# Regrouping the down side's high product by 32 copies inside the on-chip memory, in place of sixteen turnings on TensorE

## The chip, the cores and the metric

The kernel runs on one core of a Trainium2 chip. The metric is the device time of one execution in microseconds (us), lower is better. TensorE (PE) multiplies, VectorE (DVE), ScalarE (ACT) and GpSimd (POOL) do the rest, and SyncE (SP) issues most of the DMA transfers. A change of less than 0.3% of the time is within what repeated measurements of this kernel can tell from no change.

## The reference, cut to what matters

```
def butterfly(y, weights, dim):            # 11 stages for dim 2048
    for stage in range(weights.shape[0]):
        s = 2 ** stage
        nb = dim // (2 * s)
        yr = y.reshape(*lead, nb, 2, s)
        a, b = yr[..., 0, :], yr[..., 1, :]
        w = weights[stage].reshape(nb, s, 2, 2)
        y = jnp.stack([w00 * a + w01 * b, w10 * a + w11 * b], axis=-2).reshape(*lead, dim)
    return y
...
h = einsum('bsd,dh->bsh', layernorm(x), W_exp) + b_exp
h = butterfly(h, up_weights, 2048)
h = gelu(h + up_bias)
h = butterfly(h, down_weights, 2048)
y = einsum('bsh,hd->bsd', h, W_con) + b_con + down_bias
```

x has shape (32, 512, 512). Ahead of this stands a gate: x is multiplied, after a layernorm, by a decaying running sum of the squared context, and added to x. Both butterflies are linear, so the kernel folds them once, at its start, into the two weight matrices: the up side into W_exp, the down side into W_con. The change touches the folding of the down side alone.

## The kernel before, in words

The kernel has two parts. The **folding** makes W1 (the up side) and W2 (the down side), both split into a rounded high half and a low remainder, so that three fast products give nearly the precision of fp32. The **main loop** then runs over 16 pairs of token blocks (`supers`), each with 8 steps `p` of 7 products by W1 (`product`, line 1916 of the profile) and the down products by W2 (`down_a`, line 1937, and `down_b`, line 1950). The first step of the first pair, `p = 0`, is woven into the end of the folding.

A butterfly of 11 stages is a product by a "low" matrix (7 stages, inside a block of 128 features) and one by a "high" matrix (4 stages, across the 16 blocks). On the down side W_con comes into the tile `wcon` with its rows in the order that the high product needs: partition (k e), slot r, for feature 128k + 16e + r. The folding steps are listed in `FOLD`; each makes one PSUM bank of 128x512 on PE (`fold_step` of the tensor block), which ACT or DVE then evicts to the place that `kept` names. Four banks are used in turn, so a step waits until the one four places ahead of it in `FOLD` is evicted. The steps that matter here are:

- `turn_high` (4 steps, line 1816) turns the down side's high matrix in `HX[:, 1]`.
- `high_dn` (16 steps, line 1818) multiplies `wcon[:, r]` by it, four products of 128 columns for each r, with W_con as the stationary side. The result is W_con turned, d on the partitions, and ACT scatters it into `Z` (viewed as `Zd`).
- `back` (16 steps, line 1824) turns each block k of `Zd` back, and the eviction writes it over `wcon[:, k]`: now the partition is the feature inside block k. These are the sixteen turnings.
- `turn_low` (4 steps, line 1820) turns the low matrix `LX[:, 1]`.
- `low_dn` (16 steps, line 1803, in the order `W2_ORDER`) multiplies block k by it. ACT rounds the result (`w2_slot`, line 992), DVE makes the remainder (line 1341), and SP stores the pair to HBM (`store_w2`, line 634).
- `bias_low` and `bias_turn` (lines 1792 and 1798) fold the biases; POOL goes on from them.
- `tokens` (8 steps, line 1822) turns the first eight 128-row blocks of normalised tokens into `raw`. DVE makes the tokens' sums in `raw` (`token_sum`, line 1462), ACT rounds a half of `raw` into a place of `xop` (`tokens_hi`, line 1040), DVE makes its remainder (`tokens_lo`, line 1445), and `product` reads both.

The tiles of the folding and those of the main loop share memory: the seven places of `xop`, 8 KB of each partition, lie over `Z` (places 0 to 3, four r each), over `HX` (4 and 5) and over `LX[:, 0]` (6). W1's own first two steps are staged in `w1_first`, a place of `xop` and `w1r` (`weights_hi`, line 1022), and SP stores them to HBM with `store_w1` (line 623), three groups for each of the two. `w1_first` lies under `raw`, so ACT waits for the stores of groups 0 and 1 before it evicts the first `tokens`.

What sets the order is the text of each engine's program, its semaphores, and SP's one queue, which issues the transfers in program order and stands still at each wait.

Of the kernel before, what the change touches and what calls it, by code (L numbers as in the profile page):

```python
# [24 lines left out]
def xattn_ffn_program(nc, x_in, ctx_in, w_exp, b_exp, up_w, up_bias, down_w, w_con, b_con, down_bias, out):  # L25
# [31 lines left out]
    XORDER = (0, 1, 3, 2, 5, 4, 6)  # L57

# [6 lines left out]
    W2_ORDER = (2, 3, 4, 5, 6, 7, 12, 13, 8, 1, 9, 0, 14, 10, 11, 15)  # L65
    W2_USE = [(i, 0) for i in range(14)] + [(3, 1), (14, 0)]
# [16 lines left out]
    with es:  # L83
# [122 lines left out]

        low_loaded = [sem("low_up_loaded"), sem("low_dn_loaded")]
# [118 lines left out]
        FOLD += [("high_dn", r, "act") for r in range(4)]  # L326
        FOLD += [("bias_low", 0, "act")]
        FOLD += [("high_dn", r, "act") for r in range(4, 8)]
        FOLD += [("bias_turn", 0, "act")]
        FOLD += [("high_dn", r, "act") for r in range(8, R - 3)]  # L330
        FOLD += [("tokens", i, "act") for i in range(2)]
        FOLD += [("high_dn", r, "act") for r in range(R - 3, R)]
        FOLD += [("tokens", i, "act") for i in range(2, J)]
        FOLD += [("turn_low", q, "act") for q in range(KH // 4)]
# [85 lines left out]
        Zd = Z[:, :, :].rearrange("p a b -> p (a b)").rearrange("p (c h) -> p c h", c=KD)  # L420

        def kept(kind, i, bank):
# [13 lines left out]
            if kind == "turn_high":  # L436
                return HX[:, 1, 4 * i:4 * i + 4, :].rearrange("p a b -> p (a b)"), whole
            if kind == "high_dn":
                return Zd[:, :, :].rearrange("p c (k r e) -> p c k r e", k=KH, r=R)[:, :, :, i, :],\
                    whole.rearrange("p (c k e) -> p c k e", c=KD, e=E)  # L440
# [3 lines left out]
            if kind == "tokens":  # L444
                return raw[:, i // J, :, :].rearrange("p c (g j i) -> p c g j i", g=G, j=J)[:, :, :, i % J, :],\
                    whole.rearrange("p (c g i) -> p c g i", c=KD, g=G)
            assert kind == "back"
            return wcon[:, i, :], whole
# [121 lines left out]
        def _(sp):  # L570
# [48 lines left out]
            def store_w1(n):  # L619
                p = W1_ORDER[n]  # L620
                for g, (m0, m1) in enumerate(GROUPS):
# [19 lines left out]
            store_w1(0)  # L641
# [338 lines left out]
        def _(act):  # L980
# [43 lines left out]
            def tokens_hi(u, m, first):  # L1024
                if not first:
                    act.wait_ge(m_done, u * PER + (m + 1 - NM))
                if m in (0, 1):
                    if first:
                        act.wait_ge(fold_made, fold_at("back", KH - 1) + 1)
# [10 lines left out]
                act.activation(xop[:, XPOS[m], 0, :, :], x_source(m), ACT.Copy).then_inc(xhi_ready, 1)  # L1040
# [48 lines left out]
            fold_step("high_dn", 3)  # L1089
            fold_step("bias_low", 0)  # L1090
            for r in range(4, 8):
                fold_step("high_dn", r)
            fold_step("bias_turn", 0)
            for r in range(8, 12):
                fold_step("high_dn", r)
            fold_step("high_dn", 12)
            for group in range(2):
                act.wait_ge(w1_stored[0][group], NX)
            for i in range(2):
                fold_step("tokens", i)  # L1100
            for r in range(13, R):
                fold_step("high_dn", r)
            for i in range(2, J):
                fold_step("tokens", i)
            for q in range(KH // 4):
                fold_step("turn_low", q)
            for k in range(4):
                fold_step("back", k)
            for k in range(4, 10):
                fold_step("back", k)  # L1110
            for i in range(J, J + 2):
                fold_step("tokens", i)
            for k in (10, 12, 14, 15):
                fold_step("back", k)
            tokens_hi(0, 0, True)
            tokens_hi(0, 1, True)
            for k in range(4):
# [123 lines left out]
        def _(dve):  # L1241
# [73 lines left out]
            def top_products(dn):  # L1315
                dve.wait_ge(path_product, spreads(dn, LOWS - 1))
                for c, bank in enumerate(TOP_PLACE[dn]):
# [3 lines left out]
                    if dn:  # L1321
                        last = nc.vector.tensor_tensor(
                            out=whole.rearrange("p o (r a e) -> p o a e r", r=R, a=2),
                            in0=paths.rearrange("p (o e r) -> p o e r", o=KH // 4, r=R).unsqueeze(2)
                            .to_broadcast([P, KH // 4, 2, E // 2, R]),
                            in1=coef.rearrange("p o a (e r) -> p o a e r", r=R), op=ALU.mult)
                    else:
                        last = path_stage(nc.vector, flat(whole), paths, coef, LOW - 1)
# [114 lines left out]
            def tokens_lo(u, m):  # L1443
                dve.wait_ge(xhi_ready, u * NM + (XPOS[m] + 1))
                nc.vector.tensor_tensor(out=xop[:, XPOS[m], 1, :, :], in0=x_source(m),  # L1445
                                        in1=xop[:, XPOS[m], 0, :, :].bitcast(f32), op=ALU.subtract).then_inc(xlo_ready, 1)
# [61 lines left out]
            for k in (11, 13):  # L1508
                fold_step("back", k)
            for i in range(J + 2, 2 * J):  # L1510
                fold_step("tokens", i)
            tokens_lo(0, 0)
            tokens_lo(0, 1)
            token_sum(0, 0, first=True)
            for k in range(2):
                fold_step("low_dn", k)
            token_sum(0, 1)
# [183 lines left out]
        def _(pe):  # L1701
# [73 lines left out]
            def fold_step(kind, i):  # L1775
# [24 lines left out]
                if kind == "low_dn":  # L1800
                    k = W2_ORDER[i]
                    wait_kept(pe, "back", k)
                    nc.tensor.matmul(bank[:, :], LX[:, 1, k, :], wcon[:, k, :], start=True, stop=True)\  # L1803
                        .then_inc(fold_made, 1)
                    return
                if kind == "tokens":
                    pe.wait_ge(xn_ready, i + 1)
                for c in range(4):
# [8 lines left out]
                    elif kind == "high_dn":  # L1817
                        last = nc.tensor.matmul(o, wcon[:, i, block_c], HX[:, 1, i, :], start=True, stop=True)  # L1818
# [4 lines left out]
                    elif kind == "back":  # L1823
                        last = nc.tensor.transpose(o, Zd[:, c, i * P:(i + 1) * P], ident[:, :])  # L1824
# [36 lines left out]
            for r in range(R):  # L1861
# [4 lines left out]
                if r == 3:  # L1866
                    fold_step("bias_low", 0)
                if r == 7:
                    fold_step("bias_turn", 0)
                if r == R - 4:  # L1870
                    for i in range(2):
                        fold_step("tokens", i)
            for i in range(2, J):
                fold_step("tokens", i)
            pe.wait_ge(low_matrix_ready, 2)
            for q in range(KH // 4):
                fold_step("turn_low", q)
            wait_kept(pe, "high_dn", R - 2)
            wait_kept(pe, "high_dn", R - 1)
            for k in range(KH):  # L1880
                if k == 10:
                    for i in range(J, J + 2):
                        fold_step("tokens", i)
                fold_step("back", k)
            for i in range(J + 2, 2 * J):
# [161 lines left out]
```

## Time and profile before

| | |
|---|---|
| median of 3 runs | 2752.51 us (2751.94 to 2758.26) |
| profiled execution, its time | 2752.11 us |
| profiled execution, its span | 2750.4 us |
| PE busy | 2728.7 us, 99% of the span |
| DVE, ACT, POOL busy | 2119.6, 1132.2, 427.1 us |
| first step of the main loop that stands free of the folding (`product(1, 0)`) | starts at 139.64 us |

The span is cut by the profiler from the first to the last instruction; the execution's time is 1.7 us longer. PE is busy nearly everywhere, so what counts is when it gets to the main loop proper, and whether it waits after that.

### The profile page before, as it was taken

Reading aid. Unit: us, or ns where it says so; the run is one execution under the profiler, and the core shown is the slowest. Engines: PE = TensorE matmul, PEld = TensorE weight load, DVE = VectorE, ACT = ScalarE, POOL = GpSimd, SP = SyncE. Lnnn points to the kernel's source line nnn. Section 1 sums busy time; section 2 is a strip of 40 time slices with the busy share of each in tenths; the row PEclk is TensorE's granted clock in tenths of the full one; section 3 lists DMA queues with packets and bytes.
Section 4 is the critical chain, followed back from the end, with each engine's and each line's share of the span. In section 5 each row is a group of like instructions: output and inputs, shape, how many; then the busy total and the mean of one; then the engine's idle time right before and its main releaser. Section 6 shows DMA issues by size and latency. Waiting matters only on the chain.

```text
span 2750.4 us, 35138 instructions
## 1 busy us (share of the span) xinstructions
PE 2728.7 (99%) x12168; PEld 2251.9 (82%) x12168; DVE 2119.6 (77%) x3544; ACT 1132.2 (41%) x1731; POOL 427.1 (16%) x608
## 2 busy tenths in 40 slices
PE   8999999999999999999999999999999999999998
PEld 6788888888888888888888888888888888888887
DVE  8888887877878777787877788787787877778533
ACT  5754434344343433434343343434334343343432
POOL 5356010110101011020111101011010101102000
PEclk8999999999999999999999999999999999999999
DMA  9675956657585675857657585675758567585543
GB/s 274 244 235 171 281 165 198 200 170 224 155 231 177 181 220 161 241 153 216 194 168 222 152 249 165 194 202 171 223 156 235 172 189 213 161 242 153 187 146 100
DMA packets 288373, 535.76 MB, mean 195 GB/s; under 512 B 36854, under 2 KB 98454, under 8 KB 271046
## 3 DMA queue, kind: packets, MB, share of 16 engines
q1 hardware_dynamic: 281808, 531.05, 64.1%
q10 hardware_dynamic: 5414, 1.25, 0.3%
q8 instruction: 99, 1.62, 0.2%
q0 software_dynamic: 976, 1.22, 0.2%
q14 instruction: 76, 0.62, 0.1%
HBM read 437.96 MB, written 63.96 MB: 182 GB/s over the span
## 4 chain that ended last, share of the span: by engine, by line
PE 98%; DVE 1%; ACT 0%; issue 0%; DMA 0%; POOL 0%; DVEq 0%
PE ps L1916 44%; PE ps L1937 25%; PE ps L1950 25%; PE ps L1814 1%; PE ps L1710 1%; PE ps L1782 0%; PE ps L1818 0%; PE ps L1812 0%; PE ps L1824 0%; DMA wexp<-in_L_ffn_W_exp_dram 0%; PE ps L2022 0%; PE ps L1803 0%; DVE raw L1462 0%; DVE xop L1445 0%; PE ps L1729 0%
## 5 line engine op out<-in xcount | busy, mean ns | idle before, releaser
L1916 PE MATMUL ps<-xop,w1r 128*128 128x512 f32 x5376 | 1366.1, 389 | 2.4 <-DVE xop L1445 2.4
L1916 PEld LDWEIGHTS ps<-xop,w1r 128*128 128x128 f32 x5376 | 1009.0, 188 | 215.2 <-DVE xop L1445 3.4
L1937 PE MATMUL ps<-w2r,ghi 128*128 128x512 f32 x2048 | 630.5, 389 | 0.0
L1950 PE MATMUL ps<-w2r,ghi 128*128 128x512 f32 x2032 | 625.7, 389 | 1.1 <-DVE x L1544 1.1
L1127 ACT ACTIVATE st<-ps 128x512 f32<-128x512 f32 x384 | 229.6, 598 | 820.0 <-PE ps L1916 819.9
L1544 DVE TENSOR_TENSOR x<-ps,x 128x512 f32<-128x512 f32 x508 | 348.4, 686 | 275.1 <-PE ps L1950 272.7
L1937 PEld LDWEIGHTS ps<-w2r,ghi 128*128 128x128 f32 x2048 | 384.4, 188 | 79.9 <-DVE w2x L1341 0.2
L1950 PEld LDWEIGHTS ps<-w2r,ghi 128*128 128x128 f32 x2032 | 381.3, 188 | 81.0 <-DVE x L1544 2.0
L1562 DVE TENSOR_TENSOR g<-ps,st 128x512 f32<-128x512 f32 x384 | 262.5, 684 | 211.7 <-PE ps L1916 211.7
L1131 ACT ACTIVATE g<-g,gelu_bias 128x512 f32<-128x512 f32 x384 | 275.5, 717 | 353.0 <-DVE g L1562 352.9
L1567 DVE TENSOR_TENSOR glo<-g,ghi 128x512 fp32r<-128x512 f32 x510 | 350.9, 708 | 72.8 <-ACT ghi L1145 72.8
L1937 PE MATMUL ps<-w2r,glo 128*128 128x512 f32 x1024 | 398.3, 389 | 0.0
L1950 PE MATMUL ps<-w2r,glo 128*128 128x512 f32 x1016 | 395.2, 389 | 0.0
L1145 ACT ACTIVATE ghi<-g 128x512 fp32r<-128x512 f32 x512 | 309.8, 629 | 12.2
L1138 ACT ACTIVATE g<-ps,gelu_bias 128x512 f32<-128x512 f32 x128 | 88.2, 689 | 349.0 <-PE ps L1916 349.0
L1937 PEld LDWEIGHTS ps<-w2r,glo 128*128 128x128 f32 x1024 | 192.3, 188 | 39.8
L1950 PEld LDWEIGHTS ps<-w2r,glo 128*128 128x128 f32 x1016 | 190.8, 188 | 39.5
L836 POOL TENSOR_TENSOR x<-x,bias_row 128x512 f32<-128x512 f32 x128 | 170.0, 1332 | 244.2 <-DVE kvT L1434 218.8
L819 POOL TENSOR_TENSOR ve<-mv,eps 128x4 f32<-128x4 f32 x32 | 12.2, 382 | 1197.2 <-DVE mv L1385 1197.2
L1371 DVE TENSOR_TENSOR_SCAN kvT<-decay,kvT 128x512 f32<-128x512 f32 x128 | 159.1, 1243 | 4.4
L1445 DVE TENSOR_TENSOR xop<-raw,xop 128x1024 fp32r<-128x1024 f32 x112 | 136.6, 1232 | 0.7 <-ACT xop L1040 0.7
L827 POOL TENSOR_TENSOR ve<-mv,eps 128x1 f32<-128x1 f32 x128 | 28.2, 220 | 597.8 <-DVE mv L1413 597.8
(182 smaller groups left out, 1700.0 us busy)
## 6 DMA issues: line engine op xcount, KB each, us to landing
w1r<-w_products SPq DMA_DIRECT2D x847, 256.0 KB, 3.3
w2r<-w_split SPq DMA_DIRECT2D x126, 1024.0 KB, 5.0
x<-in_x_dram SPq DMA_DIRECT2D x128, 256.0 KB, 7.0
raw<-kv SPq DMA_DIRECT2D x480, 64.0 KB, 2.1
out_dram<-x SPq DMA_DIRECT2D x120, 256.0 KB, 4.1
kv<-in_ctx_dram SPq DMA_DIRECT2D x64, 256.0 KB, 7.4
raw<-in_ctx_dram SPq DMA_DIRECT2D x64, 256.0 KB, 5.0
w_products<-w1r SPq DMA_DIRECT2D x43, 256.0 KB, 6.9
```

Of the source, the lines that this page charges most:

```text
L836: nc.gpsimd.tensor_tensor(out=x[:, J * h + j, :], in0=x[:, J * h + j, :], in1=bias_row[:, :], op=ALU.add).then_inc(bias_added, 1)
L1127: act.activation(st[:, i, :], bank[:, :], ACT.Copy).then_inc(copied, 1)
L1131: act.activation(g32[:, q, :], g32[:, q, :], ACT.Gelu, bias=gelu_bias[:, k:k + 1])\
L1145: act.activation(ghi[:, p % 2, q, :], g32[:, q, :], ACT.Copy).then_inc(ghi_ready, 1)
L1371: nc.vector.tensor_tensor_scan(out=flat, data0=decay[:, :], data1=flat, initial=0.0, op0=ALU.mult, op1=ALU.add).then_inc(scanned, 1)
L1445: nc.vector.tensor_tensor(out=xop[:, XPOS[m], 1, :, :], in0=x_source(m), in1=xop[:, XPOS[m], 0, :, :].bitcast(f32), op=ALU.subtract).then_ ...
L1544: nc.vector.tensor_tensor(out=x[:, J + j, :], in0=ps_yb[:, :], in1=x[:, J + j, :], op=ALU.add)\
L1562: nc.vector.tensor_tensor(out=by_chunk(g32[:, q, :]), in0=by_token(bank[:, :]), in1=by_token(st[:, i, :]), op=ALU.add).then_inc(h_ready, 1)
L1567: nc.vector.tensor_tensor(out=glo[:, p % 2, q, :], in0=g32[:, q, :], in1=ghi[:, p % 2, q, :].bitcast(f32), op=ALU.subtract).then_inc(glo_r ...
L1916: last = nc.tensor.matmul(bank[:, :], w1r[:, slot, w, c * P:(c + 1) * P], xop[:, XPOS[m], v, c, :], start=(opens and i == 0), stop=(i == l ...
L1937: last = nc.tensor.matmul(ps_ya[j][:, :], g[:, p % 2, q, j * P:(j + 1) * P], w2r[:, p % 2, kk, w, :], start=(p == 0 and kk == 0 and i == 0 ...
L1950: last = nc.tensor.matmul(ps_yb[:, :], g[:, p % 2, q, j * P:(j + 1) * P], w2r[:, p % 2, kk, w, :], start=(kk == 0 and i == 0), stop=(kk == ...
```

## The change

The high product is turned round: the high matrix is now the stationary side and `wcon[:, r]` the moving one, one product of 512 columns for each r in place of four of 128. The result of step r has the new feature index on the partitions, for each r apart, and goes to `Z[:, r]` as it is. 32 DMA transfers then bring it to the places where `back` put it: one for each r and each half of the blocks, each of 64 rows of 2 KB (128 KB), read from 64 neighbouring partitions of `Z` and written to the 8 partitions r, r + 16, ..., r + 112 of `wcon`. For that the eviction of `turn_high` orders the columns of the high matrix by (half, e, k), and the low matrix's rows no longer need an order of their own. The low half of the blocks goes first, then the top half. The 16 steps `back` are gone.

The places of `xop` are given by the new table `XSLOT` (m = 0 and 1 to places 5 and 6, off `Z`), the token steps come after the whole high product and after the first two of `low_dn`, and all are evicted by ACT. The waits in their places are shown in the diff.

```
+    XSLOT = (5, 6, 1, 0, 3, 2, 4)
+    LOW_BLOCKS_FIRST = 6
...
-        FOLD += [("high_dn", r, "act") for r in range(4)]
+        FOLD += [("high_dn", r, "act") for r in range(R)]
+        FOLD += [("tokens", i, "act") for i in range(J)]
         FOLD += [("bias_low", 0, "act")]
...
-        FOLD += [("back", k, "act") for k in range(10)]
-        FOLD += [("tokens", i, "act") for i in range(J, J + 2)]
-        FOLD += [("back", k, "dve" if k in (11, 13) else "act") for k in range(10, KH)]
-        FOLD += [("tokens", i, "dve") for i in range(J + 2, 2 * J)]
-        FOLD += [("low_dn", k, "dve") for k in range(KH)]
+        FOLD += [("low_dn", k, "dve") for k in range(2)]
+        FOLD += [("tokens", i, "act") for i in range(J, 2 * J)]
+        FOLD += [("low_dn", k, "dve") for k in range(2, KH)]
...
+            def move_dn(blocks, r, moved):
+                wait_kept(sp, "high_dn", r)
+                sp.dma_start(wcon[r:P:R, blocks, :], Z[blocks.start * E:blocks.stop * E, r, :]).then_inc(moved, NX)
...
-            store_w1(0)
+            store_w1(0, range(1))
+            sp.wait_ge(fold_made, fold_at("high_dn", R // 2 - 1) + 1)
+            for r in range(R):
+                move_dn(slice(0, KH // 2), r, dn_low_moved)
+                if r == R // 2:
+                    store_w1(0, range(1, 2))
+            sp.wait_ge(fold_made, fold_at("high_dn", R - 1) + 1)
+            for r in range(R):
+                move_dn(slice(KH // 2, KH), r, dn_top_moved[r // 4])
+            store_w1(0, range(2, NG))
...
+                if first and XSLOT[m] < R // 4:
+                    act.wait_ge(dn_low_moved, R * NX)
+                    act.wait_ge(dn_top_moved[XSLOT[m]], 4 * NX)
+                if first and m == 6:
+                    act.wait_ge(w1_stored[0][2], NX)
...
                 if kind == "low_dn":
                     k = W2_ORDER[i]
-                    wait_kept(pe, "back", k)
+                    if i == 0:
+                        pe.wait_ge(dn_low_moved, R * NX)
+                    if i == LOW_BLOCKS_FIRST:
+                        for moved in dn_top_moved:
+                            pe.wait_ge(moved, 4 * NX)
...
+                if kind == "high_dn":
+                    nc.tensor.matmul(bank[:, :], HX[:, 1, i, :], wcon[:, i, :], start=True, stop=True).then_inc(fold_made, 1)
+                    return
```

The order on PE before, from the middle of the high product to the first step of the main loop that depends on the down side; `HX,wcon` is the high product, `ident,kv` the tokens, `ident,LX` turns the low matrix, `ident,Z` are the sixteen turnings, `wcon,LX` the low product and `xop,w1r` a product of the main loop:

```order
L1818 MATMUL ps<-HX,wcon 128x128 x12
L1822 MATMUL ps<-ident,kv 128x128 x8
L1820 MATMUL ps<-ident,LX 128x128 x16
L1824 MATMUL ps<-ident,Z 128x128 x40
L1822 MATMUL ps<-ident,kv 128x128 x8
L1824 MATMUL ps<-ident,Z 128x128 x24
L1822 MATMUL ps<-ident,kv 128x128 x8
L1803 MATMUL ps<-wcon,LX 128x512 x4
L1916 MATMUL ps<-xop,w1r 128x512 x6
L1803 MATMUL ps<-wcon,LX 128x512 x2
L1916 MATMUL ps<-xop,w1r 128x512 x6
L1803 MATMUL ps<-wcon,LX 128x512 x2
```

The same place on PE with the change, from the first of the high product (`wcon,HX` now):

```order
L1798 MATMUL ps<-wcon,HX 128x512 x16
L1814 MATMUL ps<-ident,kv 128x128 x16
L1779 MATMUL ps<-LX,scr 16x128 x16
L1812 MATMUL ps<-ident,LX 128x128 x16
L1785 MATMUL ps<-ident,scr 128x16
L1794 MATMUL ps<-wcon,LX 128x512 x2
L1814 MATMUL ps<-ident,kv 128x128 x16
L1794 MATMUL ps<-wcon,LX 128x512 x2
L1897 MATMUL ps<-xop,w1r 128x512 x12
L1794 MATMUL ps<-wcon,LX 128x512 x4
L1897 MATMUL ps<-xop,w1r 128x512 x6
```

The 64 turnings of `Z` are gone, the bias products stand behind the high product instead of inside it, and the seventh low product, the first that reads a top block, stands as the third of the four in the last row but one.

SP's queue before, from the stores of W1 on (`w_first`, `xop` and `w1r` are where W1 is staged, `w_split` is W2 in HBM):

```order
L639 DMA w_folded<-W1f 128x3072 x2
L623 DMA w_products<-w_first 128x2x512
L623 DMA w_products<-w_first 128x512
L623 DMA w_products<-xop 128x4x512
L609 DMA w1r<-w_products 128x512
L623 DMA w_products<-w1r 128x2x512
L623 DMA w_products<-w1r 128x512
L623 DMA w_products<-w1r 128x4x512
L634 DMA w_split<-w2s 128x2x512
```

SP's queue with the change, over the same stretch:

```order
L636 DMA w_folded<-W1f 128x3072 x2
L620 DMA w_products<-w_first 128x2x512
L613 DMA wcon<-Z 8x8x512 x9
L620 DMA w_products<-w_first 128x512
L613 DMA wcon<-Z 8x8x512 x23
L620 DMA w_products<-xop 128x4x512
L601 DMA w1r<-w_products 128x512
L620 DMA w_products<-w1r 128x2x512
L620 DMA w_products<-w1r 128x512
L620 DMA w_products<-w1r 128x4x512
L631 DMA w_split<-w2s 128x2x512
```

The 32 moves stand between the first group of the first W1 store and the rest; the second group stands behind nine of them, and everything else behind all 32.

## Rows read from the trace of the kernel before

**Rows 1.** The page: the span, then busy time, share and instructions of each engine.

```profile
span 2750.4 us, 35138 instructions
PE 2728.7 (99%) x12168; PEld 2251.9 (82%) x12168; DVE 2119.6 (77%) x3544; ACT 1132.2 (41%) x1731; POOL 427.1 (16%) x608
```

**Rows 2.** Windows: stretch, its length, PE, PEld, DVE, ACT, POOL busy, PEclk, DMA share, GB/s.

```profile
98.00:116.00 18.00, 18.00 (x130) 14.77 (x129) 12.41 (x22) 16.63 (x32) 8.68 (x31) 1.00 0.00 1
116.00:126.00 10.00, 8.01 (x24) 4.01 (x23) 9.54 (x13) 4.38 (x7) 0.00 (x0) 1.00 0.77 284
126.00:140.00 14.00, 12.72 (x43) 7.53 (x42) 12.53 (x16) 11.58 (x19) 5.80 (x4) 1.00 0.99 306
140.00:2750.00 2610.00, 2602.25 (x11478) 2154.32 (x11476) 1997.72 (x3343) 1037.90 (x1578) 364.43 (x495) 1.00 0.64 191
```

**Rows 3.** The chain that ended last, 76 to 150 us: start, length, what.

```profile
82.97 0.49 ACT Z L995
83.51 3.67 PE ps L1792 x32
...
101.94 4.60 PE ps L1824 x40
...
107.53 2.89 PE ps L1824 x24
...
110.89 1.29 DVE raw L1345 x2
...
114.36 1.22 DVE raw L1462
...
119.70 1.14 PE ps L1803 x2
...
121.36 1.06 ACT xop L1040
122.44 1.24 DVE xop L1445
123.72 1.67 PE ps L1916 x6
...
139.64 1.61 PE ps L1916 x6
```

**Rows 4.** PE's timeline at the first low products (each is recorded as two matmuls).

```profile
111.12 3.60 PE L1803 MATMUL ps<-wcon,LX 128*128 128x512 f32 x8
```

**Rows 5.** ACT's timeline: evictions of the high product (start, length, instruction, idle before).

```profile
87.03 0.58 ACT L995 ACTIVATE Z<-ps 128x512 f32<-128x512 f32 x1
...
95.81 0.60 ACT L995 ACTIVATE Z<-ps 128x512 f32<-128x512 f32 x1 [0.30 <-PE ps L1818]
```

**Rows 6.** DVE's timeline: normalised tokens, and the first remainders of tokens.

```profile
102.25 1.91 DVE L1434 TENSOR_SCALAR kv<-x,mv,rstd 128x512 f32<-128x512 f32 x4
...
112.09 2.35 DVE L1445 TENSOR_TENSOR xop<-raw,xop 128x1024 fp32r<-128x1024 f32 x2
```

**Rows 7.** SP's queue in time: when it issued the stores of W1 and W2.

```profile
77.99 0.80 SPq L639 DMA_DIRECT2D w_folded<-W1f  x2
...
88.67 3.58 SPq L623 DMA_DIRECT2D w_products<-w1r  x3
116.21 6.12 SPq L634 DMA_DIRECT2D w_split<-w2s  x5
```

**Rows 8.** Windows at three kinds of transfer, columns as in Rows 2.

```profile
28.00:32.00 4.00, 3.22 (x8) 1.44 (x8) 3.75 (x6) 2.01 (x4) 0.00 (x0) 1.00 1.07 216
82.00:86.00 4.00, 3.59 (x33) 3.13 (x33) 3.93 (x6) 3.57 (x7) 3.84 (x4) 1.00 1.06 442
264.00:270.00 6.00, 6.00 (x29) 4.95 (x27) 3.83 (x5) 1.58 (x3) 6.00 (x6) 1.00 0.43 102
```

**Rows 9.** Line 566, the copies inside the on-chip memory: issue time min/median/max, then landing.

```profile
L566 SPq DMA_DIRECT2D raw<-kv x480: 585/601/1977, 204.3 to 2557.2; - x160
...
DMA to landing us min/median/max: 2.0/2.1/5.6
```

**Rows 10.** POOL's timeline: the first late weights of the main loop.

```profile
147.94 0.84 POOL L916 TENSOR_TENSOR scr<-late_low 128x256 f32<-128x256 f32 x1 [7.41 <-DMA late_low<-w_folded]
```

More of the change, by code:

```diff
@@ L205, in xattn_ffn_program @@
         ps_f = ps[5:8]
+        dn_low_moved = sem("dn_low_moved")
+        dn_top_moved = [sem(f"dn_top_moved{q}") for q in range(R // 4)]
         low_loaded = [sem("low_up_loaded"), sem("low_dn_loaded")]
@@ L443, in kept @@
                     whole.rearrange("p (a e r) -> p a r e", a=4, e=E)
[L444 to L448, printed above, removed]
+            assert kind == "tokens"
+            return raw[:, i // J, :, :].rearrange("p c (g j i) -> p c g j i", g=G, j=J)[:, :, :, i % J, :],\
+                whole.rearrange("p (c g i) -> p c g i", c=KD, g=G)
         def w2_slot(i):
@@ L1039, in tokens_hi @@
                     act.wait_ge(xsum_ready, u * 4 + {3: 1, 4: 2, 2: 3, 6: 4}[m])
-                act.activation(xop[:, XPOS[m], 0, :, :], x_source(m), ACT.Copy).then_inc(xhi_ready, 1)
+                act.activation(xop[:, XSLOT[m], 0, :, :], x_source(m), ACT.Copy).then_inc(xhi_ready, 1)
             def top_hi(dn):
@@ L1088, in _ @@
             weights_hi(1)
-            fold_step("high_dn", 3)
-            fold_step("bias_low", 0)
-            for r in range(4, 8):
+            for r in range(3, R):
                 fold_step("high_dn", r)
[L1093 to L1096, printed above, removed]
             for group in range(2):
                 act.wait_ge(w1_stored[0][group], NX)
-            for i in range(2):
+            for i in range(J):
                 fold_step("tokens", i)
[L1101 to L1104, printed above, removed]
+            tokens_hi(0, 0, True)
+            fold_step("bias_low", 0)
+            tokens_hi(0, 1, True)
             for q in range(KH // 4):
                 fold_step("turn_low", q)
[L1107 to L1111, printed above, removed]
-                fold_step("tokens", i)
[L1113 to L1117, printed above, removed]
+            fold_step("bias_turn", 0)
+            for k in range(2):
+                fold_step("low_dn", k)
+            for i in range(J, 2 * J):
+                fold_step("tokens", i)
+            for k in range(2, 4):
                 fold_step("low_dn", k)
@@ L1320, in top_products @@
                     coef = spread_view(ps[bank][:, :], 0, LOW - 1, KH // 4)
[L1321 to L1328, printed above, removed]
+                    last = path_stage(nc.vector, flat(whole), paths, coef, LOW - 1)
                 last.then_inc(low_matrix_ready, 1)
@@ L1507, in _ @@
                 normalise(0, 1, xs[0], j)
[L1508 to L1511, printed above, removed]
             tokens_lo(0, 0)
             tokens_lo(0, 1)
-            token_sum(0, 0, first=True)
             for k in range(2):
                 fold_step("low_dn", k)
+            token_sum(0, 0, first=True)
             token_sum(0, 1)
@@ L1865, in _ @@
                 fold_step("high_dn", r)
[L1866 to L1873, printed above, removed]
+            for i in range(J):
                 fold_step("tokens", i)
+            fold_step("bias_low", 0)
             pe.wait_ge(low_matrix_ready, 2)
@@ L1877, in _ @@
                 fold_step("turn_low", q)
[L1878 to L1885, printed above, removed]
+            fold_step("bias_turn", 0)
+            wait_kept(pe, "turn_low", KH // 4 - 1)
+            for k in range(2):
+                fold_step("low_dn", k)
+            for i in range(J, 2 * J):
                 fold_step("tokens", i)
-            wait_kept(pe, "turn_low", KH // 4 - 1)
             def product(u, p, m, first):
@@ L1915, in product @@
                 for i, (w, v, c) in enumerate(terms):
-                    last = nc.tensor.matmul(bank[:, :], w1r[:, slot, w, c * P:(c + 1) * P], xop[:, XPOS[m], v, c, :],
+                    last = nc.tensor.matmul(bank[:, :], w1r[:, slot, w, c * P:(c + 1) * P], xop[:, XSLOT[m], v, c, :],
                                             start=(opens and i == 0), stop=(i == len(terms) - 1), skip_group_check=True)
@@ L1967, in body @@
                 if first:
-                    for k in range(4):
+                    for k in range(2, 4):
                         fold_step("low_dn", k)
                     product(u, 0, 0, first)
-                    for k in range(4, 6):
-                        fold_step("low_dn", k)
                     product(u, 0, 1, first)
-                    for k in range(6, 8):
+                    for k in range(4, 8):
                         fold_step("low_dn", k)
```

28 lines of the change are left out of this document (9 added, 19 removed).

## The prediction

> **What bounds the kernel now.** I read the page first: PE is busy 99% of a span of 2750.4 us [rows 1]. Then the windows by stage: behind 140 us PE is busy 2602.25 of 2610 us, so the main loop is PE's alone and the change leaves it as it is [rows 2]. Whatever the change is worth must therefore show in one number, the start of `product(1, 0)` at 139.64 us, and the rest follows at its old length unless a transfer comes late. Third the chain that ended last, from 83 us to there [rows 3]. From 83.51 to about 111 it is PE: bias products, high product, tokens, turnings. From 110.89 to 123.72 it runs over DVE and ACT, the two engines that make the token operands, and PE waits for them: it is busy 8.01 us of the 10 between 116 and 126 [rows 2]. From 123.72 to 139.64 it is PE again with small waits. The reader should see one more thing: from 98 to 116 us the DMA engines do nothing at all (share 0.00), and from 126 to 140 they are full (0.99) [rows 2].
>
> **What the change removes.** 64 turnings on PE: 4.60 + 2.89 = 7.5 us of the chain [rows 3]. Two of their evictions and two of the tokens' leave DVE, whose first token remainders started at 112.09 although its tokens were normalised at 102.25 + 1.91 = 104.16 [rows 6]: at most 7.9 us to be gained there.
>
> **What it leaves as long.** A low product of 512 columns takes 3.60 / 4 = 0.90 us [rows 4]; the high product's four of 128 columns came every 0.90 us too (an eviction of 0.60 after 0.30 idle [rows 5]). I take 0.90 for the new high step. Evictions keep their size, 0.5 to 0.6 us, strided or not.
>
> **What it adds on PE.** The bias products (3.67 us) stood where ACT was not ready: ACT evicts the fourth high step only at 87.03 [rows 3, 5], behind the W1 rounding. Now PE makes steps 4, 5 and 6 from 83.51 on (2.7 us, to 86.2) and stands still until the fourth bank is free at 87.6: 1.4 us lost. Nine steps of 0.90 follow: the high product is made at 95.7, kept at 96.3.
>
> **The moves.** SP may issue the first when step 7 is made, 88.5. The stores ahead of it are done by then (3 MB issued at 78 [rows 7], at 442 GB/s [rows 8]). Data runs, I estimate, 1 us after issue (half of the 2.1 us in which a 64 KB copy lands [rows 9]), from 89.6. No row shows a copy to 8 partitions, so I bound it from the windows [rows 8]. Transfers over 128 partitions run at 442 GB/s. Token loads to 32 partitions run at 216 with the DMA engines full. The existing copies inside the memory, 32 partitions to 32, move 102 GB/s at share 0.43, so 237 at full share. A quarter of the partitions halves the rate. The bounds for 8 partitions: no further loss, 237 GB/s, 131 KB in 0.56 us (issuing costs 0.60 [rows 9], which then binds); or in proportion to the partitions, 59 GB/s, 2.2 us. Between ends so far apart I take the same step once more, a quarter of the partitions for half the rate: 118 GB/s, **1.11 us a move**.
>
> The Trainium skill speaks of this and against the change: "SBUF — State Buffer", section on Door 1 (the DMA port swizzle), says that bandwidth goes by how many of 16 ports the partitions reach, 0 to 31 reaching 8, about 27 GB/s each. The halving at 32 partitions agrees with it. By its table, the partitions r, r + 16, ..., r + 112 reach 4 ports: 109 GB/s, an estimate of 1.20 us a move, which would end 2.9 us later than the sum below.
>
> **Low half.** 89.6 + 16 x 1.11 = 107.4, plus 0.6 for the W1 group among them (0.26 MB at 442), 108.0, landed at about 108.7. That group lies behind nine moves, so it lands near 101, and ACT waits for it before it evicts tokens that PE made by 97.5: tokens to 103, a token rounding (1.06) to 104, the bias and a second rounding, the four low-matrix banks to about 109. Both roads let the first low product start at 109.2, against 111.12 [rows 4]. It is 1.9 us early. With tokens behind the first two low products, the last token is kept at 113.8, and the token sums start there, against 114.36 [rows 3]: the gain of 7.9 on DVE is already spent on waiting for copies and banks.
>
> **Top half.** 108.0 + 16 x 1.11 = 125.8, landed 126.5. Of the first six low products none needs it; with two token steps' worth of work and `product` 0 and 1, PE would come to the seventh at 119.5. It waits until 126.6, where the chain had it at 119.70 [rows 3]: **6.9 us late**. Behind it on ACT stands the rounding of m = 2 (before at 121.36), behind that DVE's remainder (122.44), and on it waits `product` 2 (123.72) [rows 3]. So these three shift by the same 6.9, and from there to 139.64 the order is the old one, mostly PE's own work, which I let shift whole.
>
> **Transfers behind the moves.** 2.9 MB of W1 stores, before issued by 92.3 [rows 7], now start at 126: 7 us at 442 GB/s, to 133. Five W2 stores issued from 116.21 on follow to about 139, and ACT's wait for the first three comes at about 140. The late weights landed at 147.94, POOL having stood 7.41 us for them [rows 10]; PE first needs them at about 160. They may land 5 us later against PE's own shift, which this cover holds. I add nothing; with the cover gone it is 1 to 3 us.
>
> **Sum.** The profiled execution took 2752.1 us, 1.7 more than its span and 0.4 under the median of the runs: 2752.1 + 6.9 = 2759.0, and with half a microsecond for landing tails at quarters' ends 2759.5.
>
> **The rivals.** *The moves are as fast as the existing copies* (the end on the other side). At 0.60 us a move, bound by SP's issuing, the low half is there at 100 and the top half at 110, ahead of any need. Then PE's own order decides: first low product at 104.6 (ACT's low-matrix banks), seventh at 114.8, in place of 119.70: 4.9 us gained, 2747. [...] Against it: only 8 partitions receive. *The same, and DVE catches up the rest*: the whole 7.9 us, 2744. The decision point is where the seventh low product starts at 119.70: 119.7 - 0.7 - 0.6 - 89.6 = 28.8 us for 32 moves, **0.90 us a move**. *Between*, 0.75 to 1.0 us: shift -4 to +3, 2748 to 2755. *In proportion to the partitions*, 2.2 us a move: the top half at 161, +41, 2793; the step from 128 to 32 partitions did not go in proportion, which speaks against it. *The port table's price*, 1.20 us, plus 1 to 3 us for late weights: 2763 to 2765. *The change does not do what it says*, the turnings being free anyway: the chain shows them on it, so I give this nothing.
>
> **How the numbers follow.** The slow copies (1.05 to 1.3 us a move, with the port table's case in it): 0.57, giving 2757 to 2766; 0.3% above the median is 2760.8, and a little over half of this case lies beyond. Between: 0.13. As fast as the existing copies: 0.25, of which 0.07 with DVE's catching up, near 2744.3, the edge of 0.3%. In proportion: 0.05. Slower by over 0.3%: 0.57 x 0.6 + 0.05 = 0.39; faster by over 0.3%: 0.07 less a part, 0.06; within: 0.55. The range takes in the fast copies and the slow ones with late weights: 2745 to 2767. The slow case alone: 2756 to 2766. (A shift of 0.3%, 8 us, is about what a measurement of this kernel tells from no change.)
>
> **What would show it.** The moves: the DMA window from 90 to 126 at 110 to 120 GB/s, against 230. PE idle before the seventh low product, released by a DMA into `wcon`, some 7 us. The first low product near 109. ACT idle before the first token eviction near 101, released by the W1 store. `product(1, 0)` at 146.5. DMA share full from 126 on and the late weights landing past 155. The prediction is wrong if a move takes under 0.9 us, or if SP's program issues them so late that issuing binds, or if the W1 stores behind them stop PE in step 1.

## The result, and the profile after

The changed kernel takes **2769.65 us** (median of 4 runs, 2766.84 to 2771.22) against 2752.23 for the kernel before beside it on the same chip: ratio **1.0059, 95% interval 1.0043 to 1.0075**. It is 17.4 us slower. Forecast were 2759.5 and a range of 2745 to 2767, with "within 0.3%" as the likeliest case: the direction of 2759.5 was right, the size was not, and the time lies outside the range.

The page of the changed kernel, line for line against [rows 1]:

```profile
span 2767.9 us, 34825 instructions
PE 2728.7 (99%) x12008; PEld 2239.7 (81%) x12008; DVE 2115.8 (76%) x3540; ACT 1126.5 (41%) x1719; POOL 432.8 (16%) x608
```

PE is busy for exactly as long as before, although 160 fewer matmuls are recorded. Part of what it does in the stage of the change now runs at a lower clock, as the windows show (columns as in Rows 2), and the DMA share says when the copies run and what they leave behind:

```profile
104.00:108.00 4.00, 2.93 (x14) 2.08 (x15) 0.84 (x2) 3.12 (x5) 0.00 (x0) 0.50 0.53 115
108.00:112.00 4.00, 4.00 (x27) 3.00 (x25) 0.83 (x1) 0.66 (x2) 0.00 (x0) 0.70 0.53 116
...
128.00:132.00 4.00, 0.76 (x1) 0.50 (x2) 0.00 (x0) 0.00 (x0) 0.00 (x0) 0.50 0.79 270
...
116.00:192.00 76.00, 66.59 (x264) 47.85 (x262) 55.71 (x83) 38.22 (x63) 23.61 (x37) 0.96 1.00 299
```

Where the DMA engines were idle, 98 to 116 [rows 2], they now move about 115 GB/s at half share; and from 116 to 192 their mean share is 1.00, with a dip to 0.79 in 128 to 132. PE's timeline in the same stretch (start, length, instruction, idle time before it and its releaser):

```profile
84.81 2.81 PE L1798 MATMUL ps<-wcon,HX 128*128 128x512 f32 x6 [0.87 <-ACT Z L1001]
89.17 7.96 PE L1798 MATMUL ps<-wcon,HX 128*128 128x512 f32 x18 [1.55 <-ACT Z L1001]
...
105.07 6.24 PE L1779 MATMUL ps<-LX,scr 128*16 128x128 f32 x32 [6.19 <-ACT raw L1001]
...
114.52 1.98 PE L1794 MATMUL ps<-wcon,LX 128*128 128x512 f32 x4 [1.16 <-ACT LX L1001]
...
131.24 3.45 PE L1794 MATMUL ps<-wcon,LX 128*128 128x512 f32 x4 [6.47 <-DMA wcon<-Z]
136.18 1.67 PE L1897 MATMUL ps<-xop,w1r 128*128 128x512 f32 x6 [1.49 <-DVE xop L1436]
```

The seventh low product starts at 131.24 (before 119.70), `product(1, 0)` at 152.11 (before 139.64). The chain names what comes behind that, the late weights of steps 2 and 3, and three timelines show how the second of them stops PE: ACT stands 8.89 us for them with the activations of the running step behind it, DVE waits 4.56 for `ghi`, and only then frees the bank that PE wants:

```profile
154.54 11.98 DMA late_low<-w_folded
...
178.90 12.99 DMA late_low<-w_folded
```

```profile
191.97 0.72 ACT L1154 ACTIVATE w1r<-late_top 128x256 fp32r<-128x256 f32 x2 [8.89 <-DMA late_low<-w_folded]
192.60 0.71 ACT L1129 ACTIVATE g<-g,gelu_bias 128x512 f32<-128x512 f32 x1
193.34 0.63 ACT L1143 ACTIVATE ghi<-g 128x512 fp32r<-128x512 f32 x1
```

```profile
194.00 0.72 DVE L1554 TENSOR_TENSOR glo<-g,ghi 128x512 fp32r<-128x512 f32 x1 [4.56 <-ACT ghi L1143]
194.65 0.68 DVE L1531 TENSOR_TENSOR x<-ps,x 128x512 f32<-128x512 f32 x1
```

```profile
195.38 0.97 PE L1931 MATMUL ps<-w2r,ghi 128*128 128x512 f32 x2 [3.44 <-DVE x L1531]
```

Behind that wait PE runs at the lower clock again, 0.50 in 196 to 199, which in the window around it shows as 0.83:

```profile
190.00:200.00 10.00, 6.57 (x22) 4.94 (x21) 5.54 (x10) 5.84 (x13) 7.81 (x11) 0.83 0.23 57
```

What takes PE 2.72 us at the full clock (182.26 to 184.98) takes it 4.45 us here (195.38 to 199.83). So this one stop costs 3.44 us of standing still and 1.7 us of slow work.

**How a span is read here.** From each trace three moments suffice (one trace for each kernel, so differences of a few tenths are not to be read): the start of the high matrices' turning (line 1810, `ps<-ident,HX`), the start of `product(1, 0)`, and the end. They cut the span into a start, the folding stage, and the rest. The start differs by up to 2 us between profiles of kernels whose program up to there is the same, and isn't explained by any edit. A fourth moment is the first use of the late weights of step 3 by POOL, counted from `product(1, 0)`. Times in us:

```
kernel          start   folding   rest     late weights behind product(1, 0)   span
before          77.17    62.47   2610.8    34.2                                2750.4
after           78.13    73.98   2615.8    39.9                                2767.9
g1_first        76.95    73.60   2616.3    40.8                                2766.8
ports2          77.17    83.28   2614.1    38.9                                2774.5
ports8          78.51    62.73   2615.0    40.2                                2756.2
half_rows       76.12    57.86   2619.4    42.7                                2753.4
all_first       77.29    80.05   2610.3    35.0                                2767.6
half_all        76.79    62.14   2610.5    34.6                                2749.4
via_hbm         76.29    65.43   2611.9    36.3                                2753.6
ports8_all      79.74    66.27   2610.0    35.0                                2756.0
before_w1_late  77.93    61.98   2613.9    38.4                                2753.8
before_x_late   76.65    62.55   2609.7    32.7                                2748.9
after_x_late    76.00    73.28   2610.3    33.5                                2759.6
half_x_late     77.17    59.56   2611.3    34.7                                2748.0
```

For the change: 17.5 us of span = 1.0 of start + 11.5 of folding + 5.0 of rest. The rest is 2609.7 to 2611.3 in each kernel whose late weights come up to 35 us behind `product(1, 0)`, and beyond that it grows by about a microsecond for each.

### The profile page after: what moved, and what is told of

Same layout as the page of the kernel before. It is cut to its first block, busy times and chain, and to the rows that moved or that the text cites. A ratio compares the mean times of both kernels' runs of the same rounds, so it can differ in the third digit from the quotient of the medians.

```text
span 2767.9 us, 34825 instructions
## 1 busy us (share of the span) xinstructions
PE 2728.7 (99%) x12008; PEld 2239.7 (81%) x12008; DVE 2115.8 (76%) x3540; ACT 1126.5 (41%) x1719; POOL 432.8 (16%) x608
## 4 chain that ended last, share of the span: by engine, by line
PE 95%; DMA 2%; POOL 1%; ACT 1%; DVE 0%; issue 0%; SPq 0%; ACTq 0%; DVEq 0%
PE ps L1897 43%; PE ps L1918 25%; PE ps L1931 25%; DMA late_low<-w_folded 1%; DMA wcon<-Z 1%; PE ps L1808 1%; PE ps L1769 0%; PE ps L1697 0%; DMA wexp<-in_L_ffn_W_exp_dram 0%; PE ps L1806 0%; DMA w_products<-w_first 0%; PE ps L1794 0%; POOL w1r L933 0%; PE ps L1798 0%; PE ps L1779 0%
```

## The experiments

Twelve kernels ran. Their expectations name theories by letters. Of the folding: **A**, the price of a copy is set by how many ports of the on-chip memory the receiving partitions reach; **B**, copies to 8 partitions are slow wherever these lie; **C**, the place of the W1 stores in SP's queue sets it; **D**, it is PE's wait and low clock ahead of the bias products; **E**, a fixed time per copy. Of the rest: **F**, copies and the transfers behind them are one serial resource, and the end of it sets the late weights; **G**, only the wait ahead of the seventh low product counts; **H**, half_rows lost its gain for another reason. Later **J**: bytes issued behind the folding keep the engines full until past the late weights of step 3. **K, L, M** are its rivals, told where they stand.

**ports8.** The copy `r` goes to eight partitions four apart, which by the port table of the Trainium skill reach 8 ports in place of 4. VectorE's last product writes its columns in the matching order, as eight small products in place of one.

```diff
-                sp.dma_start(wcon[r:P:R, blocks, :], Z[...])
+                first = 32 * (r // 4) + r % 4
+                sp.dma_start(wcon[first:32 * (r // 4) + 32:4, blocks, :], Z[...])
...
```

> The copies go to other partitions: step r = 4h + i writes the eight partitions 32h + i, 32h + 4 + i, ..., 32h + 28 + i, and the rows of the low matrix are put in the same order (eight small DVE products a bank in place of one). Bytes, rows of 2 KB, number of copies, order and waits stay. Theory A (the price of a copy is set by which partitions receive: in the change they fall two and two on four ports by the table of the Trainium skill, here on eight): each copy takes 0.60 to 0.65 us in place of 1.22, the last lands by about 113, the seventh low product waits for no DMA, the late weights land without a backlog, time 2747 to 2753 us. Theory B (eight receiving partitions are slow wherever they lie): nothing changes, 1.2 us a copy, 2769 to 2772 us. Theory C (SP's order costs the time, the stores of W1 behind the copies): 2767 to 2771 us too, with fast copies.

Measured: 2757.5 us, ratio 1.0019 (1.0009 to 1.0028). **ports2** sends copy `r` to the partitions `8r` to `8r + 7`, two ports by the same table, again with the low matrix in the matching order:

```diff
+                sp.dma_start(wcon[E * r:E * r + E, blocks, :], Z[...])
```

> The copies go to the eight neighbouring partitions 8r to 8r + 7, and the low matrix has its columns in that order, as in the kernel before. Bytes, rows, copies, order and waits stay. Theory A: by the table these eight fall on two ports, four and four; a copy takes 2.4 us, the top half lands near 170, the seventh low product starts some 40 us later than with the change, time 2805 to 2820 us. Theory B: 1.2 us a copy as before, 2768 to 2772 us. A third outcome, neighbouring copies overlapping on different ports, would lie between.

Measured: 2778.34, ratio 1.0093 (1.0076 to 1.011). The windows of ports2, of the changed kernel and of ports8, from 104 to 112 us, in this order:

```profile
104.00:112.00 8.00, 1.19 (x6) 0.86 (x7) 0.14 (x1) 1.84 (x4) 0.00 (x0) 0.50 0.54 90
```

```profile
104.00:112.00 8.00, 6.93 (x39) 5.08 (x40) 1.67 (x2) 3.78 (x7) 0.00 (x0) 0.60 0.53 115
```

```profile
104.00:112.00 8.00, 6.74 (x47) 4.92 (x45) 5.37 (x8) 5.38 (x13) 3.79 (x20) 1.00 0.49 171
```

The same bytes, rows of the same size and the same queue, and 90, 115 and 171 GB/s: which eight partitions receive decides the rate. **A stands in its order, B and E fall.** The seventh low product starts at 119.71 in ports8 and 139.59 in ports2. A's sizes don't hold. It gave ports8 0.60 to 0.65 us a copy and 2747 to 2753 us; the copies took 0.84 (first issued at 90.44, reckoned as below) and the kernel 2757.5. It gave ports2 2.4 us a copy and 2805 to 2820 us; 1.51 and 2778.34 were measured, which is where the third outcome lies. That neighbouring copies overlap there is likely but not shown by itself.

ports8 folds as fast as before (62.73 against 62.47) and still ends 5 us later: its rest is 2615.0. C and D said nothing of that either. From the seventh low product to `product(1, 0)` ports8 took 21.5 us, where the kernel before took 19.9; its granted clock stood at 0.74 and 0.77 in 123 to 126 and 126 to 130.

**g1_first.** Group 1 of W1 is stored ahead of the copies, so that ACT need not wait for it:

```diff
-            store_w1(0, range(1))
+            store_w1(0, range(2))
```

> Only SP's order changes: the second group of the first W1 store (256 KB) goes ahead of the 32 copies in place of behind nine of them. Theory A (the top half's landing sets the end of the folding): ACT evicts the first tokens at about 98.5 in place of 104.4, PE does not cool down before the bias products, which take 3.7 us in place of 6.2, the first low product comes 4 to 5 us earlier, and all of it is lost again before the seventh, which starts within 1 us of where it did: 2768 to 2771 us. Rival D (the 6.2 us that PE stood before the bias products, and the 2.6 us of half clock in them, are part of the loss): 2761 to 2764 us.

Measured: 2768.63, ratio 1.0057 (1.0042 to 1.0072). The bias products now start at 97.61 without a wait and take 3.67 us, not 6.24, and it buys nothing: PE waits 7.57 for the first low product's rows and 6.36 for the seventh's. **D falls**: a wait of 6.2 us and 2.6 us of slow clock, both to be read in the trace, lay in front of a later wait that absorbed them. C, for this one store, falls too.

**half_rows.** Each copy moves only 256 of 512 columns, so half of the down side's high product is missing from the output:

```diff
+                sp.dma_start(wcon[r:P:R, blocks, 0:D // 2], Z[..., 0:D // 2])
```

> Each copy carries the first 256 of its 512 columns, 64 rows of 1 KB; the other half of W2 is left as loaded, which leaves that part of the work out. Theory A (bytes through the receiving ports): 0.6 us a copy, where SP's issuing at 0.60 binds, and no wait before the seventh low product: 2746 to 2752 us. Rival E (a copy costs a fixed time for its 64 rows or its completion, not for its bytes): 1.2 us a copy, 2768 to 2771 us.

Measured: 2753.96, ratio 1.0003 (0.9993 to 1.0012), 2 us above what A gave and far from E's. The 32 copies went out in 22.4 us (88.26 to 110.63), so E falls here once more. The folding is 4.6 us shorter than before, as the forecast's fast case said (4.9), and the rest 8.6 us longer. So the time behind `product(1, 0)` is a second cost of the change, with a cause of its own. The next four kernels look for it.

**all_first** issues all W1 stores and the load of slot 7 ahead of the copies, as the kernel before does:

```diff
+            store_w1(0)
+            sp.wait_ge(w1_stored[0][0], NX)
+            load_w1(RING - 1, RING - 1)
+            store_w1(1)
             sp.wait_ge(fold_made, fold_at("high_dn", R // 2 - 1) + 1)
...
```

> Only SP's order changes: all six stores of W1's first two steps and the reload of slot 7 (3.9 MB) go ahead of the 32 copies. Theory F (the DMA engines that carry the copies are one serial resource, full from 91 to 192 us, and the late weights of step 3 that land at its end are what PE waits for): the copies start near 97 and end near 136, the seventh low product starts some 5 us later than with the change, but the backlog behind is smaller, the late weights of step 3 land within 3 us of 192, and the time stays at 2767 to 2771 us. Rival G (the wait before the seventh low product decides alone): 5 us more, 2773 to 2776 us.

Measured: 2771.1, ratio 1.0072 (1.0055 to 1.0088), 0.1 above F's range. F's other figures came too: the seventh low product starts at 136.47, 5.2 us later, and the late weights of step 3 are used at 192.30. But they are no longer what PE waits for, as F had it: behind `product(1, 0)` the rest is 2610.3, its old length, and the folding is 6.1 us longer. PE's first wait:

```profile
117.45 3.75 PE L1791 MATMUL ps<-wcon,LX 128*128 128x512 f32 x4 [13.79 <-DMA wcon<-Z]
```

**G falls**, since it kept the 5 us of the rest and came out at 2773 to 2776. The W1 stores cost some 6 us ahead of the copies and 5 behind them. **half_all** is half_rows with this order (half of the columns missing), **ports8_all** is ports8 with it.

> The copies carry 256 of 512 columns, as in half_rows, so half of the down side's high product is left out of W2, and the W1 stores go ahead of them. Theory F: the copies end by 117, nothing of theirs is waited for, and 2 MB of copies is all that the engines carry beyond the kernel before, in time in which they were idle; the late weights of step 3 land at 170 or earlier, there is no wait of PE at 176, and the 5 us that the folding gains arrive in the end: 2746 to 2749 us. Rival H (half_rows lost its gain of 5.7 us for another reason than the stores behind the copies, for instance the order of the tokens): 2752 to 2755 us as there.

> The copies to partitions a step of 4 apart (as in ports8, 0.88 us each there), with all W1 stores ahead of them. The copies run from 97 to about 125, the seventh low product starts near 126 (119.7 in ports8). Theory F: the late weights of step 3 land up to 3 us earlier than in ports8 (181.4), time 2754 to 2758 us, the same as ports8 or a little less. Rival G: the seventh product's 6 us are added, 2763 us.

Measured: half_all 2751.89, ratio 1.0000 (0.9991 to 1.0009); ports8_all 2756.39, ratio 1.0016 (1.0006 to 1.0025). In both the rest is back (2610.5 and 2610.0), and the folding pays: 62.14 against 57.86, 66.27 against 62.73. half_all missed the 2746 to 2749 of F; ports8_all lies in F's 2754 to 2758. Against H: what half_rows had lost behind the folding did come back by the order of stores alone.

**via_hbm** stores each high step to HBM as it is made and loads the matrix back in two loads of 2 MB over 128 partitions; group 1 of W1 goes ahead of that, as in g1_first:

```diff
+                sp.dma_start(dn_dram[:, :, r].rearrange("h e k d -> (h e) k d"), Z[:, r, :])
+                sp.dma_start(wcon[:, blocks, :]..., dn_dram[half_of]...)
```

> The 32 copies are replaced: each high step is stored whole to HBM (128 partitions, 256 KB, 16 stores), and when all have landed two loads of 2 MB over 128 partitions bring it back regrouped, the low half first. Twice the bytes, but over all 16 DMA engines at 400 to 437 GB/s: stores done by 100, low half landed by 106 to 108, top half by 112 to 114. The places of xop over Z are free once the stores have landed. Theory F: the seventh low product waits for nothing or under 1 us, W1's stores end near 121, and the time is 2746 to 2752 us. If instead the bytes through HBM are what counts (8.4 MB in place of 4.2), 2760 to 2768 us.

Measured: 2755.14, ratio 1.0011 (1.0002 to 1.0021); the expected 2746 to 2752 is missed. The loads are issued at 101.91, behind the last of the stores (84.03 to 98.50), and PE waits for the first of them:

```profile
109.77 3.75 PE L1797 MATMUL ps<-wcon,LX 128*128 128x512 f32 x4 [7.32 <-DMA wcon<-dn_high_folded]
```

Twice the bytes, at 332 GB/s in 92 to 98 and 422 in 104 to 112, beat the copies by 14.5 us and are still 0.1% slower than the kernel before.

**The four that test J.** The kernel before has no copies, so it can carry the second cost alone. **before_w1_late** moves three W1 stores (512, 256 and 1024 KB, so 1.8 MB and not the 3 MB of the expectation) and the load of slot 7 behind the first W2 store; L says that the cost belongs to the copies.

```diff
+            store_w2(0)
             load_w1(RING - 1, RING - 1)
             store_w1(1)
-            for i in range(5):
+            for i in range(1, 5):
                 store_w2(i)
```

> The kernel before, with no copy in it, and only three 1 MB stores of W1 and the load of slot 7 moved behind the first store of W2 (issued at about 116 in place of 88 to 92). J (bytes that are issued behind the folding keep the DMA engines full until past the late weights of step 3, ScalarE waits for those, TensorE for a bank that is freed late): product(1,0) stays at 139 to 141, the late weights of step 3 land at 177 to 180 in place of 173.9, the time is 2755 to 2758. L (the later loss of the change belongs to the copies themselves): 2751 to 2753.

Measured: 2755.69, ratio 1.0013 (1.0004 to 1.0022). `product(1, 0)` is at 139.91, the late weights at 178.26, the rest 3.1 us longer. **L falls.** The three others take 1 MB away from in front of the late weights of step 3: the second half of the next pair's `x` is loaded in step 2, behind them. K says that the time follows the landing whether or not anything waits for it, M that the late weights have nothing to do with the loss.

```diff
-                            load_x(u + 1, 1 - par)
+                            load_x(u + 1, 1 - par, (0,) if first else (0, 1))
+                        if go and first and p == 2 and m == 5:
+                            load_x(u + 1, 1 - par, (1,))
```

> The kernel before, with the second half (1 MB) of the second pair's x loads issued in step 2 behind the late weights of step 3, in place of ahead of them. J: the late weights land up to 3 us earlier, but nothing waits for them at 173.9, so no gain: 2751 to 2753. K (the time goes with the moment at which they land, whatever is waited for): 2749 to 2750.

> The changed kernel with the same edit of the x loads. J: 1 MB at 300 GB/s is 3.5 us less ahead of the late weights of step 3, which land at 188 to 189 in place of 191.9; what lies behind product(1,0) goes from 2615.8 to 2612 to 2613.5, and the time to 2766 to 2768. M (the loss behind product(1,0) has nothing to do with the late weights): 2769 to 2771.

> half_rows (half of the high product's columns are not moved, so that the output lacks them) with the same edit of the x loads. J: the late weights of step 3 land at 173 in place of 176.6, what lies behind product(1,0) goes from 2619.4 to 2615 to 2616.5, and the time from 2753.96 to 2749.5 to 2751.5. M: 2753 to 2755.

Measured: before_x_late 2751.59, ratio 1.0000 (0.9991 to 1.0008), which is J's; K's 2749 to 2750 is not reached. after_x_late **2762.7**, ratio 1.0043 (1.0029 to 1.0056). half_x_late 2749.3, ratio 0.9990 (0.9981 to 0.9999). All five times of after_x_late lie below all four of the changed kernel. **M falls**, and J was too timid: it gave 2766 to 2768 and, for the half, 2749.5 to 2751.5. For the changed kernel it gave 2 to 3.5 us, and 7 came, of which the traces put 5.5 in the rest. The traces show two things that my expectation left out. Counted from `product(1, 0)`, the late weights of step 3 are issued 1.9 us sooner and used 6.4 us sooner (in plain times 174.21 in place of 178.90, and 182.78 in place of 191.96; 2.8 us of both is the earlier `product(1, 0)` of that profile). And with the wait the 1.7 us of slow work behind it are gone too: PE's clock is 1.00 throughout 149 to 210. PE's waits behind 130 us in the changed kernel and with the moved load, in this order (engine, line, releaser: total, times, longest):

```profile
PE ps L1931 <- DVE x L1531: 4.1, 2, 3.4
```

```profile
PE ps L1933 <- DVE x L1533: 0.7, 1, 0.7
```

## Why the prediction was wrong

Point by point, by its own steps.

**What the change removes and what PE adds** held. The high steps came at 0.88 us apiece, and PE stood 2.4 us for their banks where 1.4 was given (84.81 and 89.17 above).

**The moves: slow, as forecast, but 0.09 us off 32 times, and by a rule that does not hold.** The step was "a quarter of the partitions for half the rate: 118 GB/s, **1.11 us a move**". That rule counts partitions. ports8 and ports2 have 8 receiving partitions too and moved 171 and 90 GB/s, so that 118 lay close to the 115 measured is luck. By the prediction's own reckoning the copies ran from 91.4 (first issued at 90.30) to 130.5 (0.7 ahead of the seventh low product), with 0.6 for the W1 group among them: 38.5 / 32 = 1.20 us. So 2.9 us come from the price. Another 0.8 come from the later first issue (1.8 later than forecast, of which 1.0 is the start; the rest is mostly PE's longer wait for its banks, over at 89.17 where 87.6 was forecast), and the start gives 1.0. That leads from the forecast 126.6 to 131.3; measured is 131.24. The decision point of 0.90 us a move fits ports8: its first copy went out 1.9 us later than forecast (90.44), its copies took 0.84 by the same reckoning ((119.71 - 0.7 - 91.5 - 0.6) / 32), and its seventh low product started at 119.71 against 119.70.

"SBUF — State Buffer", Door 1, in the Trainium skill gave an estimate of 1.20 us a move, and the prediction, which had this number, took the other. The trace agrees with the page for 4 ports. For 2 ports its 27.2 GB/s a port make an estimate of 54 GB/s, where ports2 shows 90 in the window above; for 8 its table gives 218, where ports8 shows 171. The order is the page's, the two other sizes are not.

**The shift behind the seventh low product**, "which I let shift whole", nearly did: 11.5 us there, 12.5 at `product(1, 0)`. The 0.9 us more arise in the seventh low product itself. PE makes it at the lower clock, and ACT can evict it 2.08 us after its start; in the kernel before it was 1.16 (119.70 to 120.86):

```profile
133.32 0.60 ACT L998 ACTIVATE w2s<-ps 128x512 fp32r<-128x512 f32 x1 [7.92 <-PE ps L1794]
```

From there everything keeps its distance: `product` 2 starts 2.86 us after each of the two evictions, and `product(1, 0)` 15.9 us after `product` 2.

**ACT's wait for the W1 group** was foreseen near 101 and ended at 104.42; PE then made the bias products at the lower clock, and the first low product came at 114.52, not 109.2. This error of 5.3 us cost nothing, since the copies were later still; g1_first shows it.

**"I add nothing; with the cover gone it is 1 to 3 us"** is the step that failed. The sum of bytes was right (late weights "past 155": they came at 166.59), but I asked when PE reads the late weights of step 2. The gate is elsewhere: ACT processes the weights of step 3 in order between the activations of the running step, so that weights that PE needs much later stop ACT now, ACT stops DVE, and DVE holds a bank. It measured 5.0 us, by the trace 3.4 of standing still and 1.7 of slow work behind it. That W1 stores issued late are enough for this, without any copy, before_w1_late shows (3.1 us); that the late weights are the gate, after_x_late shows by giving all of it back. The prediction had listed "if the W1 stores behind them stop PE in step 1"; it was step 2, and by way of ACT.

**PE's clock** has no term in the sum. The prediction let PE wait 6.9 us and go on at full speed. The granted clock fell to 0.50 at the wait ahead of the seventh low product and again at the one near 192, and that cost 0.9 and 1.7 us, both counted above.

**The chances.** Slower by over 0.3% had 0.39. The rival with the port table's price and 1 to 3 us of late weights gave 2763 to 2765; with its price, the 5.0 us measured, the 1.8 us of later start and issue and the 0.9 us on the way, the sum is 2759.0 + 2.9 + 5.0 + 1.8 + 0.9 = 2769.6, the time of the profiled execution. It must close, since the terms are differences within the same two traces; it shows how the loss is divided, and proves none of the causes.

**What stays open.** Why the start varies by 2 us and more (78.5 and 79.7 in the two ports8 kernels, whose VectorE makes eight small products at that place; the other twelve lie between 76.0 and 78.2). And what limits ports8: its 8 busy engines or its 8 ports.

**A version that beats both kernels** wasn't found. half_x_late (0.9990) leaves out half of the columns. It puts copies of half the length, once the `x` load is moved, at some 3 us.

## What to carry to other kernels

Price a copy inside the on-chip memory by the partitions that receive it, and measure one before building on it; here a stride of 4 in place of 16 was worth 12 us. When a change fills a stretch in which the DMA engines were idle, or moves stores past it, follow the queue down to the next load that an in-order engine waits for: it needn't be the load that PE reads next. And a wait on the list is only worth what no later wait absorbs; here 8.8 us ahead of the first low product were worth nothing. Where a wait does count, look at PE's clock behind it: the stop of 3.4 us cost 5.1.

## What the runs showed of the hardware

- Which 8 partitions received set the rate of the full copies: 90 GB/s for neighbours, 115 at a step of 16, 171 at a step of 4 (104 to 112 us).
- The full copies to 8 partitions ran at a DMA share of 0.49 to 0.54 at each of these rates (0.38 in half_rows, where the shorter copies went out every 0.69 us). That looks like 8 of 16 engines always busy and the other 8 without work. "DMA: Bandwidth & Descriptors", section on why a DMA increments its semaphore by 16, in the Trainium skill says that a transfer uses the largest number of engines up to 16 that divides the slowest dimension of both sides, here 8; the share agrees.
- The granted clock of PE was 0.50 (the 1.2 GHz level) in 104 to 108 us, after it had stood still for 6.2 us, in 128 to 132, with 6.5 us of standing still, and in 196 to 199, after 3.4 us. The 32 bias products took 6.24 us there and 3.67 in g1_first, where PE came to them without a pause.
- With the engines full, a 256 KB load landed 12 to 13 us after its issue (154.54 and 178.90 in the chain).
